# The second expert matmul turned round: w2 stationary, the Gelu rows in two rounded parts, gates as broadcast columns

## What is computed

```python
h = gelu(einsum('nd,edh->enh', xf, w1) + b1[:, None, :])      # E=4, 128 -> 512, exact Gelu
y = einsum('enh,ehd->end', h, w2) + b2[:, None, :]            # 512 -> 128
c = einsum('eh,ehd->ed', gelu(b1), w2) + b2
out = einsum('nk,nkd->nd', gates, y_sel - c_sel + c.sum(0))   # gates: softmax of the top 2 logits
```

## Time and profile before

| | us |
|---|---|
| median of 3 runs | 1013.58 |
| lowest, highest | 1012.38, 1014.89 |
| the profiled execution: its own time | 1014.5 |
| its span, first to last instruction | 1012.5 |
| TensorE busy | 927.7 |
| VectorE, ScalarE, GpSimd busy | 622.4, 461.4, 110.8 |

### The profile page before, as it was taken

How to read it: one execution, slowest core, us unless ns; L and a number is a source line. 1 busy time by engine, 2 the same in 40 slices (tenths; PEclk the granted TensorE clock), 3 DMA queues, 4 the chain that set the end, 5 groups by cost and what they waited for, 6 DMA issues and landing times.

```text
span 1012.5 us, 27589 instructions
## 1 busy us (share of the span) xinstructions
PE 927.7 (92%) x11035; PEld 747.4 (74%) x11035; DVE 622.4 (61%) x1971; ACT 461.4 (46%) x740; POOL 110.8 (11%) x126
## 2 busy tenths in 40 slices
PE   3583889999999999999999999999999999999996
PEld 2362667777787777777787777778787878778896
DVE  6362656757576675747576675757576675755542
ACT  1131345273635436363644537363544637363541
POOL 3210101010010001010010101011010101000000
PEclk8685679999999999999999999999999999999999
DMA  7324051332505042241505133240604133150000
GB/s 213 108 69 120 3 154 34 108 93 61 140 7 172 24 134 67 74 126 31 170 6 149 48 118 82 72 128 8 182 15 148 51 86 114 51 140 2 12 1 24
DMA packets 87259, 84.63 MB, mean 84 GB/s; under 512 B 7492, under 2 KB 81864, under 8 KB 87112
## 3 DMA queue, kind: packets, MB, share of 16 engines
q1 hardware_dynamic: 84824, 70.24, 25.1%
q0 software_dynamic: 2304, 12.58, 3.4%
HBM read 32.47 MB, written 29.36 MB: 61 GB/s over the span
## 4 chain that ended last, share of the span: by engine, by line
PE 69%; DVE 16%; issue 5%; ACT 5%; SPq 3%; DMA 2%; POOL 0%; DVEq 0%; POOLq 0%
PE y_ps L381 21%; PE s_ps L290 8%; PE o_ps L324 6%; PE s_ps L313 5%; PE s_ps L242 5%; DVE rmax L583 5%; PE s_ps L244 4%; ACT hid L854 4%; PE s_ps L243 4%; DVE x L667 3%; SPq L990 3%; PE o_ps L331 2%; PE v_ps L299 2%; PE a_ps L251 2%; PE v_ps L306 2%
## 5 line engine op out<-in xcount | busy, mean ns | idle before, releaser
L381 PE MATMUL y_ps<-w2s,hid 128*128 128x128 f32 x1920 | 270.4, 284 | 0.7
L381 PEld LDWEIGHTS y_ps<-w2s,hid 128*128 128x128 f32 x1920 | 233.5, 192 | 31.0 <-issue 19.9
L820 ACT ACTIVATE prob<-s_ps 128x1024 f32<-128x1024 f32 x128 | 131.2, 1025 | 205.9 <-PE s_ps L313 205.6
L583 DVE TRANSPOSE_TENSOR_REDUCE rmax<-s_ps 128x16 bf16<-128x512 f32 x256 | 167.6, 693 | 93.1 <-PE s_ps L290 91.9
L854 ACT ACTIVATE hid<-s_ps,b1s 128x512 f32<-128x512 f32 x256 | 170.8, 688 | 32.1 <-PE s_ps L244 31.5
L290 PE MATMUL s_ps<-qdiag,kv 64*128 64x512 f32 x768 | 137.6, 465 | 20.5 <-DMA kv<-kv_chosen 20.5
L678 DVE SCALAR_TENSOR_TENSOR x<-y_ps,gate,x 128x128 f32<-128x128 f32 x240 | 81.5, 340 | 88.9 <-PE y_ps L381 87.1
L813 ACT COPY vaug<-v_ps 128x128 f32<-128x128 f32 x128 | 34.0, 266 | 207.7 <-PE v_ps L299 205.8
L290 PEld LDWEIGHTS s_ps<-qdiag,kv 64*128 64x128 f32 x768 | 86.1, 256 | 36.3 <-issue 28.7
L242 PE MATMUL s_ps<-xn2hi,w1hi 128*128 128x512 f32 x256 | 109.2, 426 | 1.7
L244 PE MATMUL s_ps<-xn2hi,w1lo 128*128 128x512 f32 x256 | 101.0, 395 | 0.0
(11 more groups left out here) (128 smaller groups left out, 1012.3 us busy)
## 6 DMA issues: line engine op xcount, KB each, us to landing
kv_table<-stage SPq DMA_DIRECT2D x16, 768.0 KB, 3.9
kv<-stage SPq DMA_DIRECT2D x16, 768.0 KB
kv_chosen<-selected SPq DMA_DIRECT2D x16, 768.0 KB, 5.2
kv<-kv_chosen SPq DMA_DIRECT2D x16, 768.0 KB, 4.9
qdiag<-qpair SPq DMA_DIRECT2D x512, 16.0 KB
xs<-in_x SPq DMA_DIRECT2D x16, 256.0 KB, 2.8
out_x<-x SPq DMA_DIRECT2D x16, 256.0 KB, 2.3
hid<-in_w SPq DMA_DIRECT2D x1, 1024.0 KB
```

The costliest lines, as they stand in the source:

```text
L381: ins = pe.matmul(dst[:, k * P:(k + 1) * P], hid[:, e * C + c, k * P:(k + 1) * P], w2s[:, e * C + c, :], start=(c == 0), stop=(c == C - 1))
L583: v.tensor_reduce(rmax[m % 2][:, half * 8:(half + 1) * 8, :], s_ps[m % 2][:, half * N:(half + 1) * N].rearrange("p (a c) -> p a c", c=32), ...
L820: act.activation(prob[m % 2][:].rearrange("p h s -> p (h s)"), s_ps[m % 2][:], ACT.Exp, scale=SCALE).then_inc(exped, 1)
```

## The change

- **The matmul is turned.** w2 is split once into rounded w2hi and w2lo (on GpSimd, first batch) and is the stationary operand; the Gelu rows of one 128-column slice n = (e, c) of the hidden width, all 512 rows, move. A unit is now (b, n) with three rounded matmuls of 512 columns: w2hi x hi, w2lo x hi, w2hi x lo. Four units of an expert add up in the y bank. The two slots in each m stay.
- **The Gelu rows are split**: hi is a rounded copy on GpSimd (`c_hi`), lo = hid - hi on VectorE (`c_lo`), with two buffers of each in the loop and eight in the tail. The third matmul of a unit waits for lo.
- **The gates become columns.** The gates of a batch (16 x 128 after one transpose at m = 6) go to DRAM, and each expert's row of 512 comes back broadcast to 128 partitions (`put_gates`, `take_gate`, on SyncE's queue). VectorE multiplies (y + m[e]) by them, one operation of 512 columns for each expert at m = 1, 3, 5, 7 (`c_gated`); `c_constants` and the 16 adds go. GpSimd adds the experts up (`c_sum`, three a batch).
- **The sum is turned back** by four transposes in the Gelu stage at k = 8 (`c_turn`) and added to x2 in one operation (`c_add`).
- To make room, xn2 and its parts share the buffers of xn, x + bias is written in place after the rows are made (x in three buffers), and so `c_split` moves from m = 3 to m = 5. Loads of x and stores move to the start of a batch on SyncE's queue.

The diff, cut to its core:

```diff
-        w2s = sb("w2s", [P, E * C, D])
+        w2hi, w2lo = sb("w2hi", [P, E * C, D], F32R), sb("w2lo", [P, E * C, D], F32R)
...
+        NX, N2, NH, NG = 3, 3, 2, 2
...
-        xn2hi, xn2lo = sb("xn2hi", [P, N], F32R), sb("xn2lo", [P, N], F32R)
+        xn2hi, xn2lo = xnhi, xnlo
...
+        def bank_of(*use):
+            return next(of for of, _ in banks.values() if use in of.at)
+        TAIL, NT = UPS * (B - 2) + 2, 8
+        def parts_of(b, n):
+            at = UPS * b + n
+            if at < TAIL:
+                return hidhi[at % NH][:], hidlo[at % NH][:], at - NH
+            i = (at - TAIL) % NT
+            hi, lo = (q[:, i // 4, i % 4 * 2:i % 4 * 2 + 2, :].rearrange("p h s -> p (h s)") for q in qdiag)
+            return hi, lo, at - NT if at - NT >= TAIL else None
...
-            def c_down(b, e, k, bank="y"):
+            def c_down(b, n, bank="y"):
+                (of, dst), e, c = banks[bank], n // C, n % C
+                hi, lo, _ = parts_of(b, n)
+                if c == 0:
+                    was = of.next("down", b, e)
+                    if was:
+                        pe.wait_ge(of.free, was)
+                if b == 0 and n == 0:
+                    pe.wait_ge(w_split, SPLIT_W2)
+                pe.wait_ge(hi_done, UPS * b + n + 1)
+                pe.matmul(dst[:], w2hi[:, n, :], hi, start=(c == 0), stop=False)
+                pe.matmul(dst[:], w2lo[:, n, :], hi, start=False, stop=False)
+                pe.wait_ge(lo_done, UPS * b + n + 1)
+                ins = pe.matmul(dst[:], w2hi[:, n, :], lo, start=False, stop=(c == C - 1))
+                ins.then_inc(of.full if c == C - 1 else weighed, 1)
+
+            def c_gates(b):
+                was = bank_a.next("gate", b)
+                pe.wait_ge(gate_done, b + 1)
+                pe.wait_ge(bank_a.free, was)
+                pe.transpose(a_ps[0:E * T, 0:P], gate[:].rearrange("p e t -> p (e t)"), idn[:]).then_inc(bank_a.full, 1)
+
+            def c_turn(b, bank="y"):
                 of, dst = banks[bank]
-                was = of.next("down", b, e, k)
-                pe.wait_ge(gelued, UPS * b + C * (e + 1))
-                if was:
-                    pe.wait_ge(of.free, was)
-                for c in range(C):
-                    ins = pe.matmul(dst[:, k * P:(k + 1) * P], hid[:, e * C + c, k * P:(k + 1) * P],
-                                    w2s[:, e * C + c, :], start=(c == 0), stop=(c == C - 1))
+                was = of.next("turned", b)
+                pe.wait_ge(of.free, was)
+                pe.wait_ge(summed, (E - 1) * (b + 1))
+                for k in range(T):
+                    ins = pe.transpose(dst[:, k * P:(k + 1) * P], yT[:, k * P:(k + 1) * P], idn[:])
                 ins.then_inc(of.full, 1)
...
                 for m in range(M):
                     if m >= 1 and b >= 2:
                         weighted(b, m - 1)
                     row_max(b, m)
                     if m >= 1 and b < 2:
                         weighted(b, m - 1)
-                    if down:
-                        c_down(*down.pop(0))
+                    if b >= 2:
+                        c_down(b - 2, 2 * m)
                     shift(b, m)
...
-                    if down:
-                        c_down(*down.pop(0))
+                    if b >= 2:
+                        c_down(b - 2, 2 * m + 1)
                     if m + 1 < M:
...
+                    if b >= 1 and m == 6:
+                        c_gates(b - 1)
...
+                    if k == 8 and b >= 2:
+                        c_turn(b - 2)
...
+            c_columns(b)
+            c_downs(b - 1, 0, "y")
+            c_route(b, range(T))
+            c_downs(b - 1, 1, "v")
+            c_ups(0)
+            c_downs(b - 1, 2, "y")
+            c_gates(b)
+            c_ups(1)
+            c_downs(b - 1, 3, "v")
+            c_ups(2)
+            c_turn(b - 1, "y")
+            c_downs(b, 0, "v")
+            c_ups(3)
+            c_downs(b, 1, "y")
+            c_downs(b, 2, "v")
+            c_downs(b, 3, "y")
+            c_turn(b, "v")
...
-                return step(v.tensor_tensor(gate[b % 2][:], gexp[:], gsum[:].rearrange("p (t o) -> p t o", o=1).broadcast_to([P, T, E]), ALU.mult))
-
-            def c_constants(b, experts, gated):
-                i = b % N2
-                if experts[0] == 0:
-                    v.wait_ge(dve_step, gated)
-                    if b == 0:
-                        v.wait_ge(bank_a.free, bank_a.at["bias_columns", 0])
-                for e in experts:
-                    for k in range(T):
-                        if e > 0:
-                            v.wait_ge(added, (b * E + e - 1) * T + k + 1)
-                        v.scalar_tensor_tensor(x2[i][:, k, :], mcols[:, e, :], gate[b % 2][:, k, e:e + 1], x2[i][:, k, :],
-                                               ALU.mult, ALU.add).then_inc(added, 1)
-
-            def c_down(b, e, k, bank="y"):
-                i, (of, src) = b % N2, banks[bank]
-                v.wait_ge(of.full, of.at["down", b, e, k])
-                if e == 0:
-                    v.wait_ge(added, (b * E + E - 1) * T + k + 1)
-                else:
-                    last, _ = banks["yv"[k % 2]] if ("down", b, e - 1, k) in bank_v.at else banks["y"]
-                    v.wait_ge(last.free, last.at["down", b, e - 1, k])
-                v.scalar_tensor_tensor(x2[i][:, k, :], src[:, k * P:(k + 1) * P], gate[b % 2][:, k, e:e + 1], x2[i][:, k, :],
-                                       ALU.mult, ALU.add).then_inc(of.free, 1)
+                if b >= 1:
+                    v.wait_ge(bank_a.full, bank_a.at["gate", b - 1])
+                v.tensor_tensor(gate[:].rearrange("p e t -> p t e"), gexp[:],
+                                gsum[:].rearrange("p (t o) -> p t o", o=1).broadcast_to([P, T, E]), ALU.mult).then_inc(gate_done, 1)
...
+            def c_lo(b, n):
+                hi, lo, _ = parts_of(b, n)
+                v.wait_ge(hi_done, UPS * b + n + 1)
+                v.tensor_tensor(lo, hid[:, n, :], hi.bitcast(F32), ALU.subtract).then_inc(lo_done, 1)
+
+            def c_gated(b, e):
+                of, i = bank_of("down", b, e), (E * b + e) % NG
+                src = next(s for bank, s in banks.values() if bank is of)
+                v.wait_ge(of.full, of.at["down", b, e])
+                v.wait_ge(gate_in[i], 16 * times(E * b + e, NG))
+                if b == 0 and e == 0:
+                    v.wait_ge(bank_a.free, bank_a.at["bias_columns", 0])
+                if b >= 1 and e == 0:
+                    last = bank_of("turned", b - 1)
+                    v.wait_ge(last.full, last.at["turned", b - 1])
+                dst = yT if e == 0 else gate_cols[i]
+                v.scalar_tensor_tensor(dst[:], src[:], mT[:, e:e + 1], gate_cols[i][:], ALU.add, ALU.mult).then_inc(of.free, 1)
+
+            def c_add(b):
+                of, i = bank_of("turned", b), b % N2
+                src = next(s for bank, s in banks.values() if bank is of)
+                v.wait_ge(of.full, of.at["turned", b])
+                rows = x2[i][:].rearrange("p t d -> p (t d)")
+                v.tensor_tensor(rows, src[:], rows, ALU.add).then_inc(of.free, 1)
...
             for b in range(B):
-                down = down_list(b - 2) if b >= 2 else []
                 for m in range(M):
                     row_max(b, m)
-                    if down:
-                        c_down(*down.pop(0))
+                    if b >= 2:
+                        c_lo(b - 2, 2 * m + 1)
...
+                    if b >= 2 and m + 1 < M:
+                        c_lo(b - 2, 2 * m + 2)
+                    if b >= 2 and m % 2:
+                        c_gated(b - 2, m // 2)
                     if b + 1 < B:
                         if m == 1:
                             a_columns(b + 1)
-                    if b >= 1 and m == 3:
+                    if b >= 1 and m == 5:
                         c_split(b - 1)
+                    if b >= 1 and m == 6:
+                        c_gates_turned(b - 1)
...
+                if b >= 2:
+                    c_add(b - 2)
                 if b >= 1 and b + 1 < B:
                     block_max(b + 1, 0)
-            b, down = B - 1, down_list(B - 2)
-            for n in range(2):
-                c_down(*down[n], "yv"[n % 2])
+                if b >= 1:
+                    c_lo(b - 1, 0)
...
+            def c_hi(b, n):
+                g.wait_ge(gelued, UPS * b + n + 1)
+                hi, _, was = parts_of(b, n)
+                if was is None:
+                    g.wait_ge(scored, 2 * M * B)
+                elif was >= 0:
+                    b_was, n_was = divmod(was, UPS)
+                    if n_was % C == C - 1:
+                        of = bank_of("down", b_was, n_was // C)
+                        g.wait_ge(of.full, of.at["down", b_was, n_was // C])
+                    else:
+                        g.wait_ge(weighed, was - was // C + 1)
```

(63 more changed lines are left out.)

257 lines of the change are left out of this document (145 added, 112 removed).

## The result

The changed kernel takes 1117.5 us (median of 4 runs, 1115.13 to 1118.31), the kernel before 1012.98 beside it (4 runs, 1012.13 to 1014.89). The ratio is 1.1025, with a 95% interval from 1.1001 to 1.1049. The direction was forecast, the size was not: 1031 was the forecast, 1085 the upper end of the range, and 1110 the top of the highest case that was given a chance.

A forecast was written before the change was run, and what follows sets the result against it. TensorE, busy 92%, was taken as the bound, with VectorE and the chosen keys' fetch close behind. From 1014.5, 13 batches at +1.65 (+21.5) and -4 for last loop, first batches and tail gave 1032, forecast 1031; range 980 to 1085.

The forecast's parts named there:

- TensorE's units: Second expert matmul: a unit takes 0.87 us in the first slot and 0.78 in the second, 3.6 us less a batch.
- Steps 0, 3, 4 and 5: Attention loop slices m: 0.35 us less at m = 0, +0.05 at 3, -0.53 at 4, 0 at 5.
- stall of 1.64 us ahead of low part 13: At m = 6 VectorE's low part waits for GpSimd's rounding, queued behind the normed rows' low part: 1.64 us.
- growth from shift 6 to the index: End of the loop, up to the list of chosen blocks: 2.27 us becomes 3.94, +1.67.
- contention: Rival: VectorE's two-SBUF-input subtractions stall beside GpSimd at m = 1 and 6; up to 1.7 us a batch, 1054; chance 0.20.
- clock: Rival: granted TensorE clock falls at m = 6, half speed for 7 to 13 us; 4 us a batch, 1084; chance 0.14.
- collision of the rows: At m = 1 VectorE's row normalisations stand still while GpSimd rounds for unit 4: +0.45 us, bounds 0 to 1.9.
- VectorE's removed work: In the loop, 16 adds and 16 multiplications with constants go: some 9.4 us of VectorE's queue.
- The last batches: Tail: 32 units cost 0.70 instead of 0.90 us each, but a longer end follows; -1 us, from -5 to +4.
- Behind the index: From index to next scores: the gates' store on SyncE delays the chosen keys' read back 0 to 0.4 us; 0.3 taken.
- ScalarE's Gelus would hide it: Gelu stage: four transposes turning the sum back, about 0.45 us, may be hidden by Gelus nearly as long as the matmuls.
- the fetch of the chosen keys: After the index, gather, write and read back take some 17 us, a second limit before the next batch's scores.

The follow-up runs named there:

- both moves: Changed kernel with GpSimd's x + bias one slice later and its rounding for unit 13 ahead of the normed rows' low part: 1049.82 us.
- the run with three moves: Changed kernel with x + bias one slice later, rounding 13 ahead of the normed rows' low part, and SyncE's gates' store behind the chosen keys' fetch: 1042.16 us.
- the run without the split: Changed kernel with the loop's rounding and subtraction replaced by one-column operations from the third slice on, tail unchanged: 1003.4 us.
- the run with the tail's other order: Three-move kernel; in the last batch VectorE subtracts for the next expert before multiplying this one by the gates: 1038.6 us, ratio 1.0271 to before.

## Why the prediction was wrong

**Where the 104 us are.** From the third list of indices to the last, 13 stretches take 752.4 us before and 843.8 after: +91.3. Ahead of them -1.2, behind them +13.9. The forecast had +21.5 and -4.

**What held.** TensorE's units: 0.90 and 0.80 us where 0.87 and 0.78 were worked out from the earlier trace rows. Steps 0, 3, 4 and 5. The stall of 1.64 us ahead of low part 13 (1.62), and the growth from shift 6 to the index: 1.67 forecast, 1.96 measured, of which 1.27 goes when the rounding is moved. With both moves made, a batch is 1.5 us longer than before, and the forecast had 1.65; that they are so near is chance, since that kernel no longer has the stall, for which the forecast had 1.67. Without it the steps of the forecast add up to about nothing, so 1.5 us are missing even where contention and clock are mostly out of the way. They lie in steps 2 to 3 (+0.46), 5 to 6 (+0.32), from shift 6 to the index (+0.68) and behind it.

**The failed step: the contention of two-input operations and the clock stood at nothing in the sum, and were taken as alternatives.** The sum had 0.45 us a batch for the collision of the rows, nothing for `level` and nothing for the clock; the runs showed 1.0 to 1.3 us for `level` and 3.4 to 3.9 us for the clock. The chances gave contention and clock a case each, with "VectorE's subtractions of two SBUF tiles stand still too" at +1.7 a batch and the clock at +4, and the range ended inside the second. The runs show that they come together, and that the first feeds the second. The collision at slice 1 adds 1.3 us to a step in which TensorE already waits; with that wait the clock falls at slice 2 in 12 of 13 batches, without it (x + bias moved) in four, and with the wait but idle matmuls in it in three. Forecast plus both rivals, 1031 + 22 + 52, would have been 1105, 1.1% below the result. That is in part luck, since 1.7 us a batch were put on contention for two places and the tail, +13.9 instead of -1, is not in it.

**Sizes.** Contention: the rival's place and mechanism at slice 1 were right. The router's `level` took 1.24 us instead of 0.21, by the 1.28 of GpSimd's x + bias. The Trainium skill (SBUF — State Buffer, Who interferes with whom) says that a VectorE instruction with two SBUF inputs contends with a GpSimd instruction that reads SBUF. This case's traces now agree: 1.24 us in the change, 1.29 in the kernel before with one wait added. I had left the rule out of the forecast because no row showed such a pair; the earlier trace rows showed VectorE standing still under the same GpSimd operation, and was the nearest row. The forecast's own collision term, +0.45 on the rows, was 0.28 (1.39 against 1.11 us). Clock: 4 us a batch estimated, 3.9 measured, but for a fall at slice 2 and another at slices 6 and 7, where I had looked for one at slice 6; that the sizes agree is partly luck. The earlier trace rows had been read only for the slice that it resembled. One sum was wrong and without effect: VectorE's removed work, 16 x 0.34 and 2 x 2.19, is 9.8 us and not 9.4.

**The last batches.** -1 was forecast with bounds of -5 and +4, and +11.3 us came between the last Gelu and the end alone. The term was made from TensorE's work (32 units by 0.2 us less); there is no TensorE-bound work left in that stretch. Rounding, subtraction, matmuls, multiplication, sum and turning back follow each other through four engines, the subtractions at 0.9 to 1.1 us each beside GpSimd instead of 0.62. The clock has a share too: in the run with three moves the same two groups of subtractions take 4.40 and 3.57 us, but the clock falls only at 1034.1, behind the last expert matmuls, and the stretch is 24.0 instead of 25.5.

**Behind the index** 0.3 was forecast for the gates' store and +1.57 came. Moving that store on SyncE gained nothing, so the reason given was wrong. 0.9 of it is the clock: it goes with the rounding moved, and with the idle matmuls too, which leave the stall where it is (17.92 in most batches). 0.6 stays in every run with the rounding moved, and 0.35 in the run without the split. 0.44 is the turning back, which stands in the chain of work that ended last, in the periods looked at, one of the run with three moves and one of the run without the split; the chain before goes over the triples and Gelus and has no such piece. The prediction had hoped that ScalarE's Gelus would hide it. What is left, some 0.2, stays open. The chain before doesn't go over the fetch of the chosen keys either, which the prediction took for the limit there.

**What stays open.** Which of TensorE's waits brings the clock down isn't settled: a wait longer by 1 us in the kernel before did not, the changed kernel's first batch with units has the long step 1 to 2 (7.63) and no fall behind it (5.20), and the version with three moves has batches without a fall and batches with one. Whether some placement of the split makes the change faster than the kernel before is open as well; none of those tried here does.

## What to carry to other kernels

Work taken off the busiest engine is worth only what the others leave of it: here 3.0 us a batch became 1.6 without the split, and a loss once each unit needed a chain over GpSimd and VectorE. Before putting a GpSimd operation on SBUF into a loop, list what VectorE does between SBUF tiles at that moment, and count on a small one ending only with GpSimd's: 1.0 us more here where the two began together, 0.4 where it began late. And treat contention and clock as terms that add up: whatever makes TensorE wait longer in a slice that is already light can halve its clock in the next.

## What was unexpected of the hardware

VectorE's comparison of 64 columns isn't slowed by some share beside GpSimd's x + bias, it ends with it: 1.24 and 1.29 us beside 1.28, 0.59 where it began later, 0.21 alone. The brake works both ways for long series: four roundings on GpSimd take 3.67 us and four subtractions on VectorE 4.41 when they meet, 2.29 and 2.48 apart (in the run with the tail's other order). And 19 matmuls of no use in each batch made the kernel 40.8 us faster, since the granted clock stayed at 1.00 in most places where it had been 0.51: 17.1 us at half clock in 13 batches instead of 137.3.
